# Two attention layers in software-pipelined steps: projections of a group issued nearer to their use, and four buffers for the rows read back from the experts

## The reference, cut to what matters

```python
x = x + tanh(g_xattn[0]) * mha(layernorm(x), ctx, ctx, Wq, bq, Wk, bk, Wv, bv, Wo, bo)
x = x + tanh(g_ffn[0])   * top2_experts(layernorm(x))       # 8 experts, relu, 256 -> 1024 -> 256
x = x + tanh(g_xattn[1]) * masked_causal_mha(layernorm(x), ctx, ctx, mask, Wq, Wk, Wv)   # no bias, no Wo
x = x + tanh(g_ffn[1])   * sparsemixer_experts(layernorm(x))  # 8 experts, silu gate, 256 -> 512 -> 256

# mha: q, k, v = x Wq, ctx Wk, ctx Wv in 16 heads of 16;  softmax(q k' / 4) v
```

## Time and profile before

| | us |
|---|---|
| median of 3 runs | 1919.13 |
| the profiled execution, whole | 1922.39 |
| its span, first to last instruction | 1920.0 |
| TensorE busy | 1654.4 (86%) |
| VectorE busy | 1214.8 (63%) |
| ScalarE busy | 1196.7 (62%) |
| GpSimd busy | 792.0 (41%) |
| chain that ended last: TensorE | 74% |
| chain that ended last: DMA, of it `U<-ys_scr` | 7%, 5% |
| mean granted TensorE clock | 0.862 |

### The profile page before, as it was taken

The page is one execution under the profiler, slowest core; times in us unless marked ns, Lnnn a source line. Parts: engine busy times, 40 slices in busy tenths (PEclk is TensorE's granted clock), DMA queues, the critical chain, the costliest instruction groups (busy, mean ns, idle before and its releaser), DMA issues.

```text
span 1920.0 us, 35929 instructions
## 1 busy us (share of the span) xinstructions
PE 1654.4 (86%) x12316; PEld 1600.4 (83%) x12316; DVE 1214.8 (63%) x2877; ACT 1196.7 (62%) x2795; POOL 792.0 (41%) x877
## 2 busy tenths in 40 slices
PE   2799999993899999999825899999996499999990
PEld 1599999992899999999814889888996499999990
DVE  3466676635577777777544666767654666666665
ACT  1487777741788888888513656655752377777770
POOL 2123433223466666666511013322321356656650
PEclk9799999855899999999956887877965699999995
DMA  2866766602777777787527667556530477777757
GB/s 104 189 157 166 170 164 144 154 23 67 214 231 235 230 229 234 227 235 228 163 83 170 148 127 168 148 120 170 133 89 22 143 231 237 231 229 230 235 184 271
DMA packets 231014, 332.65 MB, mean 173 GB/s; under 512 B 25152, under 2 KB 168772, under 8 KB 230704
## 3 DMA queue, kind: packets, MB, share of 16 engines
q1 hardware_dynamic: 211344, 289.46, 55.9%
q0 software_dynamic: 13632, 35.13, 5.3%
q10 hardware_dynamic: 5856, 5.77, 1.0%
HBM read 253.22 MB, written 79.25 MB: 173 GB/s over the span
## 4 chain that ended last, share of the span: by engine, by line
PE 74%; DMA 7%; DVE 7%; issue 5%; POOL 3%; ACT 2%; SPq 1%; POOLq 0%; DVEq 0%; ACTq 0%
PE ps L378 16%; PE ps L380 16%; PE ps L379 16%; PE ps L497 11%; PE ps L398 6%; DMA U<-ys_scr 5%; PE ps L414 3%; POOL xs_scr L1151 2%; PE ps L507 2%; PE ps L416 1%; PE ps L423 1%; PE ps L478 1%; DVE X L930 1%; DVE X L1363 1%; DMA xs_scr<-U,PI 1%
## 5 line engine op out<-in xcount | busy, mean ns | idle before, releaser
L1055 POOL TENSOR_TENSOR KXR<-U,KXR 128x1024 fp32r<-128x1024 f32 (+1 forms) x156 | 334.6, 2145 | 306.3 <-ACT KXR L654 305.6
L378 PE MATMUL ps<-QR,KXR 128*128 128x256 f32 x1248 | 354.6, 284 | 8.5 <-DVE QR L1059 8.5
L379 PE MATMUL ps<-QR,KXR 128*128 128x256 f32 x1248 | 354.0, 284 | 0.0
L380 PE MATMUL ps<-QR,KXR 128*128 128x256 f32 x1248 | 353.7, 283 | 0.0
L654 ACT ACTIVATE KXR<-U 128x1024 fp32r<-128x1024 f32 (+1 forms) x312 | 287.7, 949 | 77.9 <-PE ps L380 62.1
L497 PEld LDWEIGHTS ps<-VA,U 128*128 128x128 f32 x2048 | 307.5, 227 | 13.2 <-DVE U L919 8.7
L497 PE MATMUL ps<-VA,U 128*128 128x17 f32 x2048 | 301.6, 282 | 5.0 <-DVE U L919 3.6
L568 ACT ACTIVATE U<-ps,mx 128x128 f32<-128x128 f32 x1024 | 295.8, 395 | 9.0 <-DVE mx L909 8.9
L378 PEld LDWEIGHTS ps<-QR,KXR 128*128 128x128 f32 x1248 | 238.0, 191 | 9.8 <-DVE QR L1059 9.8
L379 PEld LDWEIGHTS ps<-QR,KXR 128*128 128x128 f32 x1248 | 238.0, 191 | 0.0
L380 PEld LDWEIGHTS ps<-QR,KXR 128*128 128x128 f32 x1248 | 237.7, 190 | 0.0
(11 more groups left out here) (185 smaller groups left out, 3789.8 us busy)
## 6 DMA issues: line engine op xcount, KB each, us to landing
U<-in_wpack SPq DMA_DIRECT2D x234, 512.0 KB, 4.1
qk_scr<-U SPq DMA_DIRECT2D x32, 1024.0 KB, 5.0
QR<-qk_scr SPq DMA_DIRECT2D x96, 256.0 KB, 5.5
KXR<-qk_scr SPq DMA_DIRECT2D x192, 128.0 KB, 7.0
U<-xs_scr SPq DMA_DIRECT2D x78, 257.0 KB, 4.5
U<-in_wpack SPq DMA_DIRECT2D x78, 256.0 KB, 3.5
U<-in_ctx_t SPq DMA_DIRECT2D x16, 512.0 KB, 8.5
U<-ys_scr SPq DMA_DIRECT2D x32, 256.0 KB, 6.3
```

What stands on the lines that cost most here:

```text
L378: e.matmul(o, wh, xh, start=first, stop=False)
L379: e.matmul(o, wh, xl, start=False, stop=False)
L380: return e.matmul(o, wl, xh, start=False, stop=done)
L1055: e.tensor_tensor(w_cols(L, WL, n), w_raw(L, n), hi, ALU.subtract).then_inc(*l_w[n](L, i))
```

## The change

Offsets change, and nothing in the arithmetic. Per group: the transposes of x go from steps -10, -9 to -1, 0, and Q from -8, -7 to 2, 3; K goes from -1, 0 to 4, 5, and V from 4, 11 to 8, 11. With x go the statistics (-18 to -10), the reciprocal root (-14 to -6), the normalisation (-12 to -4) and the add of the experts' rows (-19 to -11). The stores of Q and K follow their projections (`Q0[1] + 1`, `K0[1] + 1`: to 4 and 6). The first stacked read goes from 3 to 8; the second stays at 12. The load of ctx goes from -8 to -7 and its rounding from -4 to -3; the loads of x in the first layer from -22 to -14. YL is loaded at -15 instead of -21, into four buffers, four steps ahead of its use instead of two, and `ON` gets memory of its own. The loop begins at step -31 instead of -38.

```diff
-FIRST, LAST = -38, 147
-X0, Q0, K0, V0 = (-10, -9), (-8, -7), (-1, 0), (4, 11)
+FIRST, LAST = -31, 147
+X0, Q0, K0, V0 = (-1, 0), (2, 3), (4, 5), (8, 11)
...
+        ON = sb("ON", [128, 2, D])
...
-        ON = U4[:, 4 * D:6 * D].rearrange("p (r d) -> p r d", r=2)
...
# ScalarE and GpSimd: rounding of ctx
-                if (g := grp(s, -4)) is not None:
+                if (g := grp(s, -3)) is not None:
...
# VectorE
-                        if (g := grp(s, -19 + j)) is not None:
+                        if (g := grp(s, -11 + j)) is not None:
                             b = g * G + j
-                            w.wait_ge(*d_yl[b % 2][b])
+                            w.wait_ge(*d_yl[b % 4][b])
...
-                    if (g := grp(s, -18 + j)) is not None:
+                    if (g := grp(s, -10 + j)) is not None:
...
-                if (g := grp(s, -14)) is not None:
+                if (g := grp(s, -6)) is not None:
...
-                    if (g := grp(s, -12 + n)) is not None:
+                    if (g := grp(s, -4 + n)) is not None:
...
# SyncE
-                if (g := grp(s, -8)) is not None:
+                if (g := grp(s, -7)) is not None:
...
-                if L == 0 and (g := grp(s, -22)) is not None and g:
+                if L == 0 and (g := grp(s, -14)) is not None and g:
                     sp_load_x(e, g)
...
-                        if (g := grp(s, -21 + j)) is not None:
+                        if (g := grp(s, -15 + j)) is not None:
                             b = g * G + j
-                            if b >= 2:
-                                w.wait_ge(*v_yl[b - 2])
+                            if b >= 4:
+                                w.wait_ge(*v_yl[b - 4])
...
-                    if (g := grp(s, (3, 12)[n])) is not None:
+                    if (g := grp(s, (8, 12)[n])) is not None:
```

More of the change, by code:

```diff
@@ L261, in program @@
         d_q = [mark(f"d_q{r}", [k + (n,) for k in halves if k[1] % 2 == r for n in range(3)], 16) for r in range(2)]
-        d_yl = [mark(f"d_yl{r}", [b for b in range(B) if b % 2 == r], 16) for r in range(2)]
+        d_yl = [mark(f"d_yl{r}", [b for b in range(B) if b % 4 == r], 16) for r in range(4)]
         d_sc = [mark(f"d_sc{r}", [(L,) + p.key + (z, j) for L in LL for p in PARTS if p.g % 2 == r for z in range(2) for j in range(p.lo, p.hi)], 16) for r in range(2)]
@@ L926, in dve_attention @@
                     for j in range(G):
-                        if (g := grp(s, -19 + j)) is not None:
+                        if (g := grp(s, -11 + j)) is not None:
                             b = g * G + j
-                            w.wait_ge(*d_yl[b % 2][b])
-                            e.scalar_tensor_tensor(X[:, b], YL[:, b % 2, 0], GT[:, 0, 0, b:b + 1], X[:, b], ALU.mult, ALU.add).then_inc(*v_c.up())
+                            w.wait_ge(*d_yl[b % 4][b])
+                            e.scalar_tensor_tensor(X[:, b], YL[:, b % 4, 0], GT[:, 0, 0, b:b + 1], X[:, b], ALU.mult, ALU.add).then_inc(*v_c.up())
                             w.wait_ge(*v_c.now)
-                            e.scalar_tensor_tensor(X[:, b], YL[:, b % 2, 1], GT[:, 0, 1, b:b + 1], X[:, b], ALU.mult, ALU.add).then_inc(*v_yl(b))
+                            e.scalar_tensor_tensor(X[:, b], YL[:, b % 4, 1], GT[:, 0, 1, b:b + 1], X[:, b], ALU.mult, ALU.add).then_inc(*v_yl(b))
                 for j in range(G):
-                    if (g := grp(s, -18 + j)) is not None:
+                    if (g := grp(s, -10 + j)) is not None:
                         b = g * G + j
@@ L1119, in pool_attention @@
             for s in range(FIRST, LAST):
-                if (g := grp(s, -4)) is not None:
+                if (g := grp(s, -3)) is not None:
                     w.wait_ge(*a_ct[L, g])
                     e.tensor_tensor(CT[:, 1], CX[:, g % 2], CT[:, 0].bitcast(F32), ALU.subtract).then_inc(*p_ct(L, g))
-                if (g := grp(s, -14)) is not None and g:
+                if (g := grp(s, -6)) is not None and g:
                     w.wait_ge(*v_st1[L, g])
@@ L1263, in sp_attention @@
                     for j in range(G):
-                        if (g := grp(s, -21 + j)) is not None:
+                        if (g := grp(s, -15 + j)) is not None:
                             b = g * G + j
-                            if b >= 2:
-                                w.wait_ge(*v_yl[b - 2])
-                            e.dma_start(YL[:, b % 2], ys_d[0].rearrange("(k b p) d -> p b k d", k=2, p=128)[:, b]).then_inc(*d_yl[b % 2](b))
+                            if b >= 4:
+                                w.wait_ge(*v_yl[b - 4])
+                            e.dma_start(YL[:, b % 4], ys_d[0].rearrange("(k b p) d -> p b k d", k=2, p=128)[:, b]).then_inc(*d_yl[b % 4](b))
                 if (g := grp(s, Q0[1] + 1)) is not None:
```

## The result

The changed kernel took 1952.45 us (median of 4 runs, 1950.5 to 1955.38), the kernel before 1921.24 (4 runs, 1917.66 to 1924.83): a ratio of 1.0164 [1.0138, 1.019], 31 us slower. I had 1931: slower, but with +12. Its profiled execution took 1955.38 us with a span of 1953.1.

The account below looks back on a forecast made before the run. TensorE was taken as the bound, alone in the first layer, with low clock and idle time in the second. First layer +28, second -16: +12 on the profiled 1922.39 us, which stands 3.3 above the median, so 1931; range 1882 to 1982.

Parts of the forecast that it names:

- the clock behind the router products: Half clock from router products to Q: 8.0 us a group, 40 per layer; in the first layer in place of 11.4.
- first rival: Busy TensorE regains its clock by itself in bare steps: 1852 us in all, chance 0.13.
- VectorE in the second layer: Second layer, steps 6 to 10: TensorE waits 2.4 us for VectorE's division, six times, 14 us.
- second rival: VectorE keeps up in the second layer, so its 14 and 21 us vanish: 1896 us, chance 0.17.
- the starts: Earlier layer starts: first scores near 60 and 1016 us; 8 us gained in the first layer, 22 in the second.
- the stacked reads: Wait for stacked K before step 12's scores: 0.5 us a group, 3 us per layer, bounds 0 to 3 a group.
- VectorE's pause: Second layer: clock lost behind TensorE's wait for the division, 3.5 us each, 21 in all, bounds 0 to 8 each.
- third rival: Stacked rows late everywhere, clock falling at step 12, three steps earlier: 5 us more per group, 1985 us, chance 0.15.
- +36: First layer's stretch, fourth step to step 110's router products: 321.7 us against 285.6, before the gain at the start.
- work (2.5 against 4.5): Group 1's projections now stand behind the first scores: 4.5 us at full clock added to each layer's stretch.

Follow-up runs that it names:

- e5: Kernel before with K at steps 2 and 3, first stacked read two steps later, V's first half one later; chip A: 1942.29 us, ratio 1.0114.
- f3: Kernel before with only YL in four buffers, loaded earlier, and ON in its own memory; chip C: 1926.9 us, ratio 0.9707.
- e4: Changed kernel plus twelve unread 240-column products in each of two steps behind the router products; chip A: 1928.19 us, 1.0024 of the kernel before.
- f2: Changed kernel, first stacked read at step 3 except in the first group, taking the previous group's rows; chip C: 1944.82 us, 0.9747 of the kernel before.
- e6: Changed kernel, first stacked read at step 3 except in the first group, taking the previous group's rows; chip B: 1949.33 us, 0.9839 of the kernel before.
- f1: Changed kernel unaltered, run again on chip C: 1958.94 us, 0.988 of the kernel before.

## Why the prediction was right or wrong

**Right: what bounds, and the clock behind the router products.** First layer: the step from router products to Q runs at half clock, L398 at 1.09 us. The size, +28.6 in the sum, is near what e5 measures for K's place alone, +25.8. The first rival falls as far as this kernel's time goes (it had 1852): TensorE was busy and the clock did not come back in the bare steps behind the router products of the changed kernel, nor in its tail. By the Trainium skill's rule ("TensorE: Matmul & The Clock Gate", section "What's actually happening") it would have. In some places the traces agree with it, two of them behind an output projection: for 2 us at 205 in the chain above, and in f3's tail. In e4, products of 240 columns one behind the other brought it back.

**Right: VectorE in the second layer.** I had 2.4 us, six times, 14 us; it is 11.1 in six waits, five of them of 2.0 to 2.1 us, once a group. The second rival falls.

**Right: the starts.** First scores at 57.59 (60) and 1016 (1016); the first layer's stretch starts 10.8 us earlier (8), and the second layer's fourth step, at 1086.87, 25.0 us once 58.2 are taken off (22).

**Wrong: the stacked reads, the step that failed.** I wrote "I take 0.5 us a group in each layer, 3 us each, between 0 and 3 us a group". They cost seven waits of 2.1 us, 14.9, in the first layer alone. My own bounds had it: 14 to 15 us from store to last byte against 13 to 14.5. I chose the end at which they just arrive and priced only the wait, not the clock behind it, though I had priced that for VectorE's pause. What I called the third rival is what happened in the first layer: the wait takes the clock two steps ahead of the router products. It also does so in group 1, which I had left at the full clock.

The stretch grew by 69.0 where I had +36. The missing 33 are 23.8 of clock (52.4 against 28.6) and 11.1 of idle time (14.1 against 3), less 2.0 of work (2.5 against 4.5). Of the clock, 13.7 (0.16 x 85.43) is missing before step 30, where I had none and where f2 and e6 show the late reads to be the cause: with the reads early the clock there is 1.00 and 0.98. In the five groups it is 37.6 more than before (0.18 x 269.19 against 0.05 x 217.21), 9 above my 28.6, and there no run shows whose these 9 are, as the clock stayed at 0.82 with the reads early.

**Too dear: the second layer.** It gave 27 us, where I had 16. In its five groups missing clock is 0.16 x 260.98 = 41.8 us against 47.4 before, where I had 61 against 62.7 for the stretch. The term that was too large is the 21 us for the clock behind VectorE's pause. One of these pauses, and what follows it:

```profile
1159.77 1.06 PE L497 MATMUL ps<-VA,U 128*128 128x17 f32 x8 [2.04 <-DVE ON L919]
...
1165.39 0.64 PE L398 MATMUL ps<-cst,U 128*128 128x128 f32 x4
```

At 1165.39, behind V, the full clock is back. From the end of the pause to the router products the five groups ran at 0.85, 0.85, 1.00, 0.73 and 1.00 for 10.2 to 12.8 us: 7 us of clock in five groups, 1.4 each instead of 3.5.

**The sum.** First layer +58.2 instead of +28, second -27 instead of -16, together +31 instead of +12. The two errors have opposite signs, so the total came out nearer than either layer, which is luck. Of the first layer's missing 30, the late reads account for 25 in the changed kernel's own windows: 11.1 of waits and 13.7 of clock before step 30. By runs they cost 14 to 25 us (f1 less f2), on chip C and with VectorE's wait in their stead, so for the first measurement no run sizes them.

## What to carry to other kernels

A dense piece of work is worth its place twice: it does its work, and it gives the small operations behind it their clock. Before moving one, look at what stands ahead of its old place (short products, a pause), and price what will run at half clock until the next one. A wait that is close to zero by two estimates is to be priced with what follows it. Here that was 2 us of wait and, where the clock had been full, some 7 us of clock (13.7 behind two waits), but at most 2 where the clock fell soon afterwards anyway. A gain that hangs on such margins of one or two microseconds is to be measured on more than one chip.

## What was not expected of the hardware

- On chips A, B and C the kernel before took 1922.3, 1974.66 and 1990.63 us, 3.6% apart; the changed one took 1952.45 in the first measurement and 1958.94 on C. With YL alone, most of what A and C differ by sits in the first layer's pauses and its clock (217.21 us at 0.95 against 264.28 at 0.82 with the same instructions), not in the work.
- In the group read, reads behind a store of 1 MB in the same queue gained 3.4 us in their issue from not waiting for it and gave 1.2 back in their landing (7.0 us against 5.8); the layer's wait for them went from 14.9 to 13.5 us in all.
- Twelve products of 240 columns, 1.5 us of work at the full clock and 2.9 at half, were enough in the rows read of e4 to have the next transposes at the full clock (0.63 us for four instead of 1.09). In f3 an output projection, six products of 256 columns, was once enough as well, and in the other tails it was not.
